# A pixel table stored once instead of twice, and gathered as two lines per tile

## The reference

```python
def _dcnv2(x, w_off, b_off, w, b, k, pad):
    om = conv(x, w_off, pad) + b_off            # offsets y, offsets x, mask: 3 * k * k channels
    sy = om[:, :P] + base_y                     # P = k * k taps
    sx = om[:, P:2 * P] + base_x
    val = _bilinear(x, sy, sx) * sigmoid(om[:, 2 * P:])[:, None]
    return einsum('ncphw,ocp->nohw', val, w) + b
h = lrelu(bn(_dcnv2(x, w_off1, b_off1, w1, b1, 1, 0)))      # 512 -> 256 channels, 1 tap
h = lrelu(bn(_dcnv2(h, w_off2, b_off2, w2, b2, 3, 1)))      # 256 -> 512 channels, 9 taps
out = x + h
```

## Time and profile before

| | |
|---|---|
| median of 3 runs | 3176.06 us (3172.43 to 3177.47) |
| the profiled execution's own time | 3181.72 us |
| its span, first to last instruction | 3179.9 us |
| stage one, about | 0 to 308 us |
| stage two, about | 308 to 665 us |
| passage to stage three, about | 665 to 712 us |
| stage three, about | 712 to 3180 us |

### The profile page before, as it was taken

The page is one execution under the profiler, slowest core; times in us unless marked ns, Lnnn a source line. Parts: engine busy times, 40 slices in busy tenths (PEclk is TensorE's granted clock), DMA queues, the critical chain, the costliest instruction groups (busy, mean ns, idle before and its releaser), DMA issues.

```text
span 3179.9 us, 52201 instructions
## 1 busy us (share of the span) xinstructions
PE 3045.7 (96%) x15660; PEld 2472.5 (78%) x15660; DVE 2755.8 (87%) x4830; ACT 2510.6 (79%) x4736; POOL 1681.7 (53%) x1701
## 2 busy tenths in 40 slices
PE   6997888989999999999999999999999999999998
PEld 6997445558888888888888888888888888888888
DVE  5545899978999998998999998999989999999987
ACT  3665677778888888888888888888888888888886
POOL 0001444456656666566566666566666665666652
PEclk8999899989999999999999999999999999999999
DMA  8998999999999999999999999999999999999994
GB/s 310 322 339 299 352 349 332 334 332 398 373 357 378 368 362 376 365 365 379 359 370 377 357 372 374 356 381 367 359 379 363 364 368 350 362 362 352 367 347 174
DMA packets 432939, 1124.82 MB, mean 354 GB/s; under 512 B 42908, under 2 KB 173084, under 8 KB 432848
## 3 DMA queue, kind: packets, MB, share of 16 engines
q0 software_dynamic: 244672, 891.09, 75.1%
q1 hardware_dynamic: 116944, 161.19, 14.4%
q10 hardware_dynamic: 71232, 71.57, 6.5%
HBM read 1003.70 MB, written 137.04 MB: 359 GB/s over the span
## 4 chain that ended last, share of the span: by engine, by line
PE 69%; DVE 17%; issue 6%; ACT 5%; DMA 2%; ACTq 1%; DVEq 0%; SPq 0%; POOLq 0%
PE psum_t L1269 49%; PE psum_t L1256 9%; PE psum_t L386 5%; PE psum_t L697 4%; DVE arena L1190 4%; DVE val_first L1198 2%; DVE z_sb L1212 2%; DVE val_lo L1205 2%; DVE arena L835 1%; ACT val_hi L1153 1%; ACT psum_t L1139 1%; DMA arena<-w 1%; ACT z_sb L1162 1%; PE psum_t L682 1%; DVE arena L859 1%
## 5 line engine op out<-in xcount | busy, mean ns | idle before, releaser
L1125 POOL DMA_INDIRECT arena<-table,plan_in x1521 | 1516.2, 997 | 968.6 <-DVE arena L1198 419.0
L1269 PE MATMUL psum_t<-val_hi,w_hi 128*128 128x512 f32 (+2 forms) x3096 | 1240.4, 401 | 1.8 <-ACT z_sb L1162 0.5
L1269 PE MATMUL psum_t<-val_hi,w_lo 128*128 128x512 f32 (+2 forms) x3096 | 1200.2, 388 | 0.0
L1269 PE MATMUL psum_t<-val_lo,w_hi 128*128 128x512 f32 (+2 forms) x3096 | 1196.8, 387 | 0.0
L1139 ACT ACTIVATE psum_t<-arena,plan_in 128x512 f32<-128x512 f32 x1521 | 1044.1, 686 | 138.2 <-DVE arena L1190 133.9
L1190 DVE SCALAR_TENSOR_TENSOR arena<-arena,plan_in,psum_t 128x512 f32<-128x512 f32 x1521 | 1123.1, 738 | 10.6 <-ACT psum_t L1139 10.5
L1269 PEld LDWEIGHTS psum_t<-val_hi,w_hi 128*128 128x128 f32 x3096 | 582.6, 188 | 137.2 <-ACT z_sb L1162 36.2
L1269 PEld LDWEIGHTS psum_t<-val_hi,w_lo 128*128 128x128 f32 x3096 | 581.7, 188 | 121.1
L1205 DVE TENSOR_TENSOR val_lo<-psum_t,val_hi 128x1024 fp32r<-128x1024 f32 (+2 forms) x387 | 465.4, 1203 | 230.4 <-ACT val_hi L1153 230.3
L1269 PEld LDWEIGHTS psum_t<-val_lo,w_hi 128*128 128x128 f32 x3096 | 583.7, 189 | 102.9
L1153 ACT ACTIVATE val_hi<-psum_t 128x1024 fp32r<-128x1024 f32 (+2 forms) x387 | 390.0, 1008 | 281.2 <-PE psum_t L1256 281.0
(11 more groups left out here) (90 smaller groups left out, 2454.7 us busy)
## 6 DMA issues: line engine op xcount, KB each, us to landing
arena<-x SPq DMA_DIRECT2D x90, 512.0 KB, 8.3
table<-arena ACTq DMA_DIRECT2D x42, 896.0 KB, 8.3
out<-arena SPq DMA_DIRECT2D x136, 256.0 KB, 4.7
table<-arena ACTq DMA_DIRECT2D x42, 768.0 KB, 7.1
arena<-x SPq DMA_DIRECT2D x70, 384.0 KB, 6.3
arena<-table,plan_in POOLq DMA_INDIRECT x1521, 6.7
table<-table SPq DMA_DIRECT2D x32, 512.0 KB, 8.8
arena<-w POOLq DMA_DIRECT2D x2, 2304.0 KB, 13.9
```

The source lines that it names most:

```text
L1125: nc.gpsimd.indirect_dma_start(landing(r, i)[:, :], None, rows, bass.IndirectOffsetOnAxis(ap=row.bitcast(u32), axis=0))\
L1269: last = nc.tensor.matmul(psum_acc[:, oc, 0:n], a[:, w, oc * P:(oc + 1) * P], b[:, r % 2, kt, 0:n], start=(w == 0 and a is w2_hi and b is ...
```

## The change

`table1` is stored once: its rows have 256 floats (1 KB), row r holds pixel r - 52. Two neighbouring rows, 2 KB in one piece, hold the two pixels of one image line. The second line of the sample begins 52 rows further. The plan makes two indices per pixel (one more DVE operation in each of its two passes, 12 linked steps in place of 11), and POOL issues two indirect DMAs for each tile, 2 KB per pixel each, into the two halves of the same slot; both raise the slot's semaphore, and ACT waits for 32 in place of 16. What the slot holds is now ordered by image line, so ACT's and DVE's operands on it are two pieces of 256 with a step between them in place of one piece of 512. `table2` and stage three are as they were.

```diff
-    table1 = nc.dram_tensor("table1", [TABLE_ROWS, 2 * C_MID], f32, kind="Internal").ap()
+    table1 = nc.dram_tensor("table1", [TABLE_ROWS, C_MID], f32, kind="Internal").ap()
...
-        gather1 = area_b[:, 0:SLOTS * 4 * C_MID].rearrange("p (s n) -> p s n", s=SLOTS)
+        gather1 = area_b[:, 0:SLOTS * 4 * C_MID].rearrange("p (s l n) -> p s l n", s=SLOTS, l=2)
...
-        index1 = part(TILES).bitcast(u32)
+        index1 = part(2 * TILES).bitcast(u32).rearrange("p (l t) -> p l t", l=2)
...
-            link(nc.vector.tensor_tensor(rows, axis(spot, 0), first, ALU.add))
+            link(nc.vector.tensor_tensor(rows(0), axis(spot, 0), first, ALU.add))
+            link(nc.vector.scalar_tensor_tensor(out=rows(1), in0=axis(spot, 0), scalar=float(WIDTH), in1=first,
+                                                op0=ALU.add, op1=ALU.add))
...
-                for table in (table1, table2):
-                    for row, col in ((0, 0), (PIXELS, C_MID)):
-                        pool.dma_start(table[row:row + WIDTH, col:col + C_MID], offsets1_flat[0:WIDTH, 0:C_MID])\
-                            .then_inc(edge_written, 16)
+                for table, row, col in ((table1, 0, 0), (table2, 0, 0), (table2, PIXELS, C_MID)):
+                    pool.dma_start(table[row:row + WIDTH, col:col + C_MID], offsets1_flat[0:WIDTH, 0:C_MID])\
+                        .then_inc(edge_written, 16)
...
-                            table_writes(act, table1, y_stage, c, half, table1_written[half])
+                            table_writes(act, table1, y_stage, c, half, table1_written[half], copies=1)
...
-                    pool.sem_inc(gather_cleared, 1)
-                    nc.gpsimd.indirect_dma_start(
-                        gather1[:, t % SLOTS, :], None,
-                        table1[0:image_end(t) + WIDTH, :], bass.IndirectOffsetOnAxis(ap=index1[:, t:t + 1], axis=0))\
-                        .then_inc(gathered[t % SLOTS], 16)
+                    for line in range(2):
+
+                        pool.sem_inc(gather_cleared, 1)
+                        nc.gpsimd.indirect_dma_start(
+                            gather1[:, t % SLOTS, line, :], None,
+                            table1[0:image_end(t) + WIDTH, :],
+                            bass.IndirectOffsetOnAxis(ap=index1[:, line, t:t + 1], axis=0))\
+                            .then_inc(gathered[t % SLOTS], 16)
...
-                    act.wait_ge(gathered[t % SLOTS], (t // SLOTS + 1) * 16)
+                    act.wait_ge(gathered[t % SLOTS], (t // SLOTS + 1) * 32)
...
-                    nc.scalar.activation(near_bank(t), gather1[:, t % SLOTS, 0:2 * C_MID], ACT.Identity,
+                    nc.scalar.activation(near_bank(t), gather1[:, t % SLOTS, :, 0:C_MID], ACT.Identity,
                                          scale=weights1[:, 0, t:t + 1]).then_inc(near_scaled, 1)
...
-                        out=gather1[:, t % SLOTS, 0:2 * C_MID], in0=gather1[:, t % SLOTS, 2 * C_MID:4 * C_MID],
+                        out=gather1[:, t % SLOTS, :, 0:C_MID], in0=gather1[:, t % SLOTS, :, C_MID:2 * C_MID],
```

More of the change, by code:

```diff
@@ L116, in deformable_kernel @@
         B_SIZE = SLOTS * 4 * C_MID + Q_SIZE
-        C_SIZE = 4265
+        C_SIZE = 4265 + TILES
         Y_SIZE = CHUNK * C_MID
@@ L372, in on_gpsimd @@
                                    .rearrange("(s p) n -> p s n", p=P)).then_inc(raw_loaded[part_no], 16)
-                pool.wait_ge(edge_written, 64)
+                pool.wait_ge(edge_written, 48)
             def on_tensor(pe):
@@ L408, in copy_y @@
                         if j == j0:
-                            act.wait_ge(table1_written[half], (c + 1) * 32)
+                            act.wait_ge(table1_written[half], (c + 1) * 16)
                     act.wait_ge(x_used, c * CHUNK + j + 1 + MOST_BACK)
@@ L440, in on_scalar @@
                 for half in range(2):
-                    act.sem_inc(table1_written[half], 32)
-                act.wait_ge(edge_written, 64)
+                    act.sem_inc(table1_written[half], 16)
+                act.wait_ge(edge_written, 48)
                 chunk(0, first=True)
@@ L517, in plan @@
                                 tile0 + 1, lambda q: weights1[:, q, tile0:tile0 + n].unsqueeze(2),
-                                index1[:, tile0:tile0 + n].unsqueeze(2), nth + 1)
+                                lambda line: index1[:, line, tile0:tile0 + n].unsqueeze(2), nth + 1)
                     assert steps[0] == PLAN_STEPS_1, steps
@@ L593, in near_bank @@
                 at = 512 * (5 + t % 2)
-                return psum_t[:, at:at + 2 * C_MID]
+                return psum_t[:, at:at + 2 * C_MID].rearrange("p (l n) -> p l n", l=2)
             def q_cols(px, n):
@@ L665, in on_gpsimd @@
                         for half in range(2):
-                            pool.wait_ge(table1_written[half], (chunks_for(t) + 1) * 32)
+                            pool.wait_ge(table1_written[half], (chunks_for(t) + 1) * 16)
                     if t >= SLOTS:
                         pool.wait_ge(sampled1, t + 1 - SLOTS)
-                    pool.sem_inc(gather_cleared, 1)
-                    nc.gpsimd.indirect_dma_start(
-                        gather1[:, t % SLOTS, :], None,
-                        table1[0:image_end(t) + WIDTH, :], bass.IndirectOffsetOnAxis(ap=index1[:, t:t + 1], axis=0))\
-                        .then_inc(gathered[t % SLOTS], 16)
+                    for line in range(2):
[5 more added lines that the diff above has]
+                            .then_inc(gathered[t % SLOTS], 16)
             def on_tensor(pe, begin_transpose):
@@ L843, in add_upper @@
                         if j == HALVES[half][0] and c == 1:
-                            dve.wait_ge(table1_written[half], (CHUNKS + 1) * 32)
+                            dve.wait_ge(table1_written[half], (CHUNKS + 1) * 16)
                         if j == HALVES[half][0] and c >= 2:
@@ L851, in add_upper @@
                     nc.vector.scalar_tensor_tensor(
-                        out=h_buf(c)[:, j, :], in0=gather1[:, t % SLOTS, 0:C_MID],
+                        out=h_buf(c)[:, j, :], in0=gather1[:, t % SLOTS, 0, 0:C_MID],
                         scalar=weights1[:, 2, t:t + 1], in1=bias_psum, op0=ALU.mult, op1=ALU.add)\
@@ L859, in add_lower @@
                     nc.vector.scalar_tensor_tensor(
-                        out=v, in0=gather1[:, t % SLOTS, C_MID:2 * C_MID],
+                        out=v, in0=gather1[:, t % SLOTS, 1, 0:C_MID],
                         scalar=weights1[:, 3, t:t + 1], in1=v, op0=ALU.mult, op1=ALU.add)\
@@ L1321, in _ @@
             go_on()
-PLAN_STEPS_1 = 11
+PLAN_STEPS_1 = 12
 def kernel(**inputs):
```

## The result

The changed kernel takes 3233.18 us, median of 4 runs (3231.58 to 3235.47), the kernel before on the same chip 3176.76 us (3172.43 to 3178.5, 4 runs): a ratio of 1.0184, 95% interval 1.0171 to 1.0196, 56.4 us slower. The forecast was 3225 us in a range of 3206 to 3246, slower. The profiled execution of the changed kernel took 3231.58 us, its span is 3229.8.

A forecast was written before the change was run, and what follows sets the result against it. VectorE bounds stage two, TensorE stage three; with two gathers POOL becomes stage two's bound. Stage two 63.9 us later less 15 us from stage one gives +48.9: 3230.6 against the profiled execution, 3225 us against the median, range 3206 to 3246.

The forecast's parts named there:

- The first rival: POOL in stage two: a gather of half the bytes is cheap, the kernel gets faster, 3161 us; chance 0.08.
- The pace: POOL in stage two: 1.27 us per gather over 321 intervals, 407.7 us where before there were 336.8.
- this rival: Stage two: VectorE's adds with both operands in SBUF hold POOL up, 150 us in all, 3375 us; chance 0.03.
- lower bound of 0.89 us per gather: POOL in stage two: L365's 588 ns plus 0.30 us between instructions, a pair 1.78 us, hidden behind VectorE.
- The tail: End of stage two, last gather's issue to last tile sampled: 5.5 us to land, about 3.0 us on ACT and VectorE.
- Stage one: One store less, less 0.5 us for the larger plan, ends this stage 15 us earlier, bounds 4 and 22.
- the two gaps: TensorE's weight loads in stage one: 0.42 and 0.50 us per chunk close with one store issue less; 10 us taken.
- The wait for w2: Stage one: VectorE's 8.05 us wait for the load of w2's second part shortens by 2 us, between 0 and 4.
- The end of the stage: Stage one: TensorE's 3.3 us idle behind a store landing after 14.26 us is all saved, bounds 0 and 5.
- the passage: Work behind stage two's last tile, into stage three: same order and same distance, so no change.
- TensorE's clock: Stage two: TensorE falls to its lower clock in the waits and becomes the bound, 3271 us; chance 0.06.
- Less is lost: Whole kernel: less is lost than the sum says, for instance only part of the pace exposed, about 3190 us; chance 0.04.

The follow-up runs named there:

- second trace of before: The unchanged kernel before, run and profiled once more for another trace: 3174.68 us, its profiled execution with a span of 3175.1 us.
- first trace of before: The profile of the unchanged kernel before that the prediction read: execution 3181.72 us, span 3179.9 us, 5.66 us above the median of the runs.

## Why the prediction was right

**The bound changed as forecast.** POOL paces stage two with two gathers per tile, waits for nothing, and VectorE and ACT wait for it. The second gather alone costs 76.8 us; half as many further gathers cost nothing. This is the step that carried the forecast. The Trainium skill's page "DMA: Bandwidth & Descriptors", section on the anatomy of one DMA, has the fixed cost mostly in the completion. The first rival did not come: the issue itself takes 0.95 us of POOL with 0.30 us between two.

**The pace was mis-sized by 1%.** 1.27 us from bursts, 1.284 measured, 4.6 us over 321 intervals. In the kernel before a gather starts at a fixed point behind L859, and 2 of the 161 begin during an operation of VectorE with both operands in SBUF. Now they fall anywhere: one in three begins during one, and one in seven is slow. I had dismissed this rival because one burst ran beside these operations at 1.255; four intervals can't show what happens to one gather in seven. With the operands in PSUM the pace is 1.255.

**The reason for the 1.27 was wrong.** I took a price by rows, from L365. Measured, 64 rows cost 0.90 us and 128 rows 0.95. The value held because it was also what the bursts showed; the lower bound of 0.89 us per gather had no ground.

**The tail was mis-sized.** I wrote that the planner's work falls into VectorE's waits and costs nothing more. For most chunks it does. For the last full one it doesn't, as VectorE's timeline of the changed kernel shows just before the last tile:

```profile
714.73 0.40 DVE L888 TENSOR_TENSOR arena<-psum_t,arena 128x234 f32<-128x234 f32 x1
...
716.91 0.28 DVE L896 TENSOR_TENSOR plan_sb<-arena 128x117 uint32<-128x117 f32 x1
717.10 0.74 DVE L839 SCALAR_TENSOR_TENSOR arena<-arena,psum_t 128x512 f32<-128x512 f32 x1
...
718.89 0.48 DVE L863 SCALAR_TENSOR_TENSOR arena<-arena 128x256 f32<-128x256 f32 x1
```

717.10 - 714.73 = 2.4 us of planning stand ahead of the last two tiles, and the last is sampled 719.4 - 708.7 = 10.6 us behind its gather, where I had 8.5.

**Stage one was right in the sum.** 13.6 to 15.8 us measured, 15 forecast. In its parts: the issue on ACT gave 20.13 - 19.00 = 1.13 us per chunk, where I had 0.92 for the two gaps. The wait for w2 fell from 8.05 to the 6.68 us of this row, 1.4 us where I had 2; it ended 2.9 us earlier, at 67.57, since the first chunks' issues come out of the time before it:

```profile
67.57 0.43 DVE L497 CAST w_hi<-arena 128x512 fp32r<-128x512 f32 x1 [6.68 <-DMA arena<-w]
```

VectorE begins on the first tile of chunk 11 at 240.5, 11.6 us earlier than the 252.1 of the second trace of before, so, less the 1.4 us of the wait for w2, the issues gave about 10.2 us up to there, where I had 10 in all. The end of the stage gave less than its 3.3 us, about 2. The store still lands after 12.14 us, and TensorE is still idle 1.5 us between 276 and 284, where the second trace of before has 1.7 us behind its store and only the first had the 3.3. The chain of the changed kernel has there:

```profile
267.66 12.14 DMA table<-arena
```

And the window is:

```profile
276.00:284.00 8.00, 6.54 (x55) 6.34 (x54) 2.86 (x5) 4.04 (x14) 2.81 (x3) 1.00 0.89 342
```

**What follows the last tile is not at the same distance.** I carried the passage over unchanged. It is 5 us shorter now. The first multiplication by w2 (the piece of 24 matmuls in the chain) begins, in the first trace of before:

```profile
695.79 7.02 PE psum_t L1269 x24
```

And in the changed kernel:

```profile
748.31 6.08 PE psum_t L1273 x24
```

That is 30.1 and 27.8 us behind the eighth gather. My reading is that TensorE, slack in a stage that POOL paces, has less left over when the last tile arrives (its last convolution ends 10.4 us behind that gather, 12.1 in the second trace of before). 2.3 us come back there and 0.9 with the shorter first piece. The other runs paced by POOL (two gathers, 64 rows, PSUM operands) have it too: their 41st gather of stage three stands 35.5 to 36.1 us behind the 13th, in those paced by VectorE 37.2 to 38.4. The last 2 us I can't place. From the eighth gather to the end of the span the eight traces paced by VectorE have 2514.1 to 2514.5 us, which is hardly any scatter, and the four paced by POOL 2509.3, 2510.7, 2512.0 and 2512.4.

**The other rivals.** TensorE's clock stayed at 0.92 over stage two, as before: nothing bound by it. "Less is lost" did not come either. The forecast of 3225 was 8 us low. Against the second trace of before, which is near its median, the table leaves 7.3 us for the pace and its base, 2.1 for the tail and 1.4 for stage one, less 5.0 for the passage: 5.8 of the 8, the rest within the scatter. That nothing was forecast for the passage was luck for the number: without its 5.0 us the forecast would have been 13 us low, still inside the range.

## What to carry to other kernels

Before splitting one gather into two, compare the issuing engine's time for both with the time that the bound engine takes per tile, from a burst in which nothing holds the issuer: below it the split was free here (for every second tile it even shortened the stage), above it every further gather was paid for, however few bytes it carried. When dropping a DMA speeds a stage up, ask whether it was its bytes or its issue; here it was the issue on the engine of the critical chain, and moving it to an idle queue gave the same gain without the loss. Take a second trace of the kernel before when terms of a few microseconds matter.

## What the runs showed of the hardware that I had not expected

- The cost of an indirect DMA on POOL hardly depends on its size: 0.94 us for 128 rows of 4 KB, 0.95 for 128 of 2 KB, 0.90 for 64 of 2 KB, and 0.30 us between two.
- Of 106 gathers that began while VectorE ran an operation with both operands in SBUF, 44 took 1.0 to 1.3 us and the others 0.95. With the second operand in PSUM slow gathers fell from 49 to 10 of 322, and the kernel by 10.3 us.
- A store issued from POOL took 0.85 to 0.98 us of POOL, and the kernel was 13.0 us faster with it, while ACT's two further issues of a chunk, 0.43 us each in the chain, cost each chunk 1.0 to 1.1 us.
- Two gathers of 2 KB in place of one of 4 KB for every second tile shortened a stage that VectorE paces, with DMA engines at a share of 0.94, from 333.6 to 336.8 us in six traces to 327.0 and 326.4 us in two.
